# Gated cross-attention with experts on one core: mask and maximum in one VectorE instruction, exponentials from SBUF, scores in mid-round, eight P buffers

## What is computed

```python
q = (layernorm(x) @ Wq.T + bq)    # 32 x 16 heads x 128 x 8
k = (ctx @ Wk.T + bk)             # 32 x 16 heads x 120 x 8
v = (ctx @ Wv.T + bv)
scores = einsum('bhqd,bhkd->bhqk', q, k) / sqrt(8)
scores = where(mask == 0, -inf, scores)      # one 128 x 120 mask for all batches and heads
attn = softmax(scores, axis=-1)
x = x + tanh(g_xattn) * (einsum('bhqk,bhkd->bhqd', attn, v) @ Wo.T + bo)
x = x + tanh(g_ffn) * experts(layernorm(x))
```

## Time and profile before

| | |
|---|---|
| median of 3 runs | 454.4 us (454.36 to 455.76) |
| span of the profiled execution | 428.0 us |
| median less that span | 26.4 us |
| attention stage, first maxima to last routing step of round 31 | 17.92 to 257.63 us |
| one steady group of four rounds (first matmul of V to that of the next group) | 109.24 to 139.10 us |

### The profile page before, as it was taken

How to read it: one execution, slowest core, us unless ns; L and a number is a source line. 1 busy time by engine, 2 the same in 40 slices (tenths; PEclk the granted TensorE clock), 3 DMA queues, 4 the chain that set the end, 5 groups by cost and what they waited for, 6 DMA issues and landing times.

```text
span 428.0 us, 12221 instructions
## 1 busy us (share of the span) xinstructions
PE 385.6 (90%) x4245; PEld 311.8 (73%) x4245; DVE 293.0 (68%) x1075; ACT 267.9 (63%) x828; POOL 256.9 (60%) x280
## 2 busy tenths in 40 slices
PE   2989999999999999999999999898999999999500
PEld 1556776877687777768777768887999999999500
DVE  4787887888788898888898987735752333333177
ACT  2367877878788887878778683323444445544254
POOL 5354536547879699698794455444677777645500
PEclk9999999999999999999999999989999999999955
DMA  3999999952000000000000186556869888885198
GB/s 83 232 266 412 412 412 395 232 109 58 21 27 15 23 20 14 28 15 16 28 16 20 35 248 220 163 164 178 224 181 294 243 295 275 288 277 181 37 311 278
DMA packets 47194, 72.20 MB, mean 169 GB/s; under 512 B 7974, under 2 KB 31662, under 8 KB 47134
## 3 DMA queue, kind: packets, MB, share of 16 engines
q1 hardware_dynamic: 42813, 62.44, 47.5%
q0 software_dynamic: 4320, 8.99, 5.9%
HBM read 41.94 MB, written 34.20 MB: 178 GB/s over the span
## 4 chain that ended last, share of the span: by engine, by line
PE 77%; DVE 9%; ACT 6%; DMA 3%; issue 3%; SPq 1%; POOL 1%; POOLq 0%; DVEq 0%; ACTq 0%
PE S L790 14%; PE S L670 7%; PE T L772 7%; PE U L772 7%; PE S L681 7%; PE O L702 6%; PE T L689 5%; PE U L689 5%; PE O L710 5%; ACT P L862 5%; DMA yg<-res 2%; PE S L796 2%; PE E L662 2%; DVE nmax L1158 1%; PE E L651 1%
## 5 line engine op out<-in xcount | busy, mean ns | idle before, releaser
L862 ACT ACTIVATE P<-S,nmax 128x120 f32<-128x120 f32 x512 | 137.1, 411 | 41.8 <-DVE nmax L1158 41.8
L1016 POOL DMA_INDIRECT zs<-z,posu x64 | 64.6, 1010 | 58.2 <-PE O L710 24.4
L1158 DVE TENSOR_REDUCE nmax<-S 128x4 f32<-128x480 f32 x128 | 75.2, 650 | 19.8 <-PE S L681 15.2
L1027 POOL DMA_INDIRECT res<-yo,dpos x71 | 68.0, 958 | 32.5 <-DVE yo L1343 17.8
L790 PEld LDWEIGHTS S<-wbuf,H 128*128 128x128 f32 x568 | 74.3, 193 | 3.4 <-issue 0.2
L790 PE MATMUL S<-wbuf,H 128*128 128x128 f32 x568 | 75.3, 277 | 0.0
L670 PE MATMUL S<-mb_r,I_r 128*128 128x480 f32 x128 | 63.7, 499 | 3.7 <-ACT P L862 2.6
L906 ACT ACTIVATE H<-T,wbuf 128x256 f32<-128x256 f32 (+1 forms) x82 | 31.7, 445 | 41.0 <-PE T L772 41.0
L906 ACT ACTIVATE H<-U,wbuf 128x256 f32<-128x256 f32 (+1 forms) x78 | 30.5, 449 | 38.5 <-PE U L772 38.4
L977 POOL TENSOR_SCALAR z<-X,mv,rstd 128x128 f32<-128x128 f32 x56 | 44.1, 793 | 10.3 <-PE O L710 7.1
L989 POOL TENSOR_SCALAR Kb<-Kt,hm 128x480 f32<-128x480 f32 x28 | 41.4, 1487 | 13.0 <-PE O L745 6.3
(11 more groups left out here) (174 smaller groups left out, 628.9 us busy)
## 6 DMA issues: line engine op xcount, KB each, us to landing
wbuf<-wpk SPq DMA_DIRECT2D x40, 578.0 KB, 4.5
zs<-zero SPq DMA_DIRECT2D x1, 17952.0 KB, 61.6
yg<-res SPq DMA_DIRECT2D x16, 256.0 KB, 4.2
zin<-zs SPq DMA_DIRECT2D x31, 132.0 KB, 4.3
wpk<-in_w SPq DMA_DIRECT2D x1, 2048.0 KB, 57.9
wpk<-in_w SPq DMA_DIRECT2D x8, 256.0 KB, 8.2
out<-X SPq DMA_DIRECT2D x16, 128.0 KB, 3.5
ctx_sb<-in_ctx SPq DMA_DIRECT2D x1, 1440.0 KB, 16.5
```

Source lines behind the costliest of these rows:

```text
L862: ins = nc.scalar.activation(P[:, n % 4, j, :], a[:, j * LK:(j + 1) * LK], ACT.Exp, bias=nmax[:, n % 4, j:j + 1])
L1016: nc.gpsimd.indirect_dma_start(out=zs, out_offset=bass.IndirectOffsetOnAxis(ap=posu[:, F, k, i:i + 1], axis=0), in_=z2[:, F % 2, i, :], in ...
L1027: nc.gpsimd.indirect_dma_start(out=res, out_offset=bass.IndirectOffsetOnAxis(ap=dpos[:, n % NDP, h:h + 1], axis=0), in_=yo[:, n % NYO, h, ...
L1158: v.tensor_reduce(nmax[:, n % 4, :], Sb[n % NHG][:, 0:HG * LK].rearrange("p (j k) -> p j k", j=HG), AX_X, ALU.max, negate=True).then_inc(m ...
```

## The change

- The mask matmuls go, with the two casts that made their operands. The first scores matmul of a bank now starts it.
- In place of `row_max`, DVE has `masked(n)`: four instructions, each (S + mask bias) x -1 written into P, 120 columns, and the minimum of these written into `nmax`. It waits for the scores and for the transposes that read this buffer of P before.
- The exponentials read and write P in SBUF, exp(-P + nmax); P and `nmax` have eight buffers. `s_free` is replaced by `p_done` (exponentials done) for the transposes and by `max_done` for the banks.
- PE issues `scores(k + 1)` after the transposes of g = 1 in round k; the first entry of a round moves behind g = 2 and the second behind g = 3. On DVE `masked` of batch k+1 stands after `unload` and the two copies, a first entry behind it. On ACT the second entry is evicted in the next round after the first exponentials, the first entry between the two copies.
- `yg` is laid into P, and the counts of `prep_dve` fall by two.

The diff without lines that only rename a wait or change a count:

```diff
@@ -74,6 +74,7 @@
 NYG = 6
 NPT = 8
+NPB = 8
 ZROW = 8 * ZW
...
@@ -271,7 +272,6 @@
 
         I = sb("I", [128, 128])
-        I_r = sb("I_r", [128, 128], F32R)
         iota_sb = sb("iota_sb", [128, NE])
...
@@ -288,7 +288,6 @@
         hm = sb("hm", [128, HG])
         mbias = sb("mbias", [128, LK])
-        mb_r = sb("mb_r", [128, LK], F32R)
         mask_i = sb("mask_i", [128, LK], I32)
...
@@ -328,8 +327,8 @@
         Vm = sb("Vm", [LK, 2, GB * HG, NHG * (32 + DK)])
         oneV = sb("oneV", [LK, NHG, 32])
-        nmax = sb("nmax", [128, 4, HG])
-        P = sb("P", [128, 4, HG, LK])
+        nmax = sb("nmax", [128, NPB, HG])
+        P = sb("P", [128, NPB, HG, LK])
         PT = sb("PT", [LK, NPT, HG * LQ])
...
@@ -380,7 +379,7 @@
         own_i = sb("own_i", [128, NDP * TH], I32)
         own = sb("own", [128, NDP, TH])
-        yg = sb("yg", [128, NYG, UB, 2, D])
+        yg = P[:].rearrange("p n j k -> p (n j k)")[:, 0:NYG * UB * 2 * D].rearrange("p (n i k d) -> p n i k d", n=NYG, i=UB, k=2)
 
...
@@ -662,31 +661,24 @@
                 last.then_inc(e_ready, 1)
 
-            def add_mask(n):
-                if n < NHG:
-                    freed(pe, FIRST[n], 0)
-                else:
-                    pe.wait_ge(s_free, n - NHG + 1)
-                mm(Sb[n % NHG][:, 0:HG * LK].rearrange("p (j k) -> p j k", j=HG), I_r[:],
-                   mb_r[:].unsqueeze(1).broadcast_to((128, HG, LK)), start=True, stop=False)
-
             def scores(k):
                 G, i = divmod(k, GB)
                 if i == 0:
                     freed(pe, "Q", G)
                     pe.wait_ge(kb_done, G + 1)
                     pe.wait_ge(kb_first, 1)
+                wait(pe, max_done, NHG * k)
                 for g in range(NHG):
                     r = slice(32 * g, 32 * g + 32)
                     mm(Sb[g][:, 0:HG * LK].rearrange("p (j k) -> p j k", j=HG), Q[r, G % 2, i * LQ:(i + 1) * LQ],
-                       Kb[r, G % 2, :, i * LK:(i + 1) * LK], start=False, stop=True,
+                       Kb[r, G % 2, :, i * LK:(i + 1) * LK], start=True, stop=True,
                        tile_position=(32 * g, 0)).then_inc(s_ready, 1)
 
             def transposes(n):
-                pe.wait_ge(s_free, n + 1)
+                pe.wait_ge(p_done, n + 1)
                 copied(pe, prior_t(n))
                 for j in range(HG):
-                    last = nc.tensor.transpose(t_bank(n)[0:LK, j * LQ:(j + 1) * LQ], P[:, n % 4, j, :], I[:])
+                    last = nc.tensor.transpose(t_bank(n)[0:LK, j * LQ:(j + 1) * LQ], P[:, n % NPB, j, :], I[:])
                 last.then_inc(t_ready, 1)
...
@@ -809,25 +801,25 @@
                 old, new = 0 <= k - 1 < B, k + 1 < B
                 first, second = entries_of(k)
-                if first:
+                if first and k >= B:
                     entries[first[0]](first[1])
                 if old:
                     values(k - 1)
                     sums(k - 1)
                 for g in range(NHG):
                     pair(ks[2 * g:2 * g + 2])
-                    if new:
-                        add_mask(NHG * (k + 1) + g)
                     if k < B:
                         transposes(NHG * k + g)
-                    if g == 1 and second:
+                    if g == 1 and new:
+                        scores(k + 1)
+                    if g == 2 and first and k < B:
+                        entries[first[0]](first[1])
+                    if g == (3 if k < B else 1) and second:
                         entries[second[0]](second[1])
                 if k == 0:
-                    pe.wait_ge(prep_dve, 16)
+                    pe.wait_ge(prep_dve, 14)
                     pe.wait_ge(b2t_done, 1)
                     mm(Ob[:, 0:D], bvb[:], wo_sb[:], start=True, stop=True).then_inc(bvo_ready, 1)
-                if new:
-                    scores(k + 1)
                 if k == OPEN:
...
@@ -837,12 +829,8 @@
             k_entry(0)
             z_entry(0)
-            pe.wait_ge(prep_dve, 5)
-            add_mask(0)
-            add_mask(1)
+            pe.wait_ge(prep_dve, 1)
             q_entry(0)
-            add_mask(2)
-            add_mask(3)
             scores(0)
...
@@ -856,12 +844,10 @@
             def exps(n):
                 act.wait_ge(max_done, n + 1)
-                wait(act, t_ready, n - 3)
-                a = Sb[n % NHG]
                 for j in range(HG):
-                    ins = nc.scalar.activation(P[:, n % 4, j, :], a[:, j * LK:(j + 1) * LK], ACT.Exp,
-                                               bias=nmax[:, n % 4, j:j + 1])
-                ins.then_inc(s_free, 1)
+                    a = P[:, n % NPB, j, :]
+                    ins = nc.scalar.activation(a, a, ACT.Exp, bias=nmax[:, n % NPB, j:j + 1], scale=-1.0)
+                ins.then_inc(p_done, 1)
 
...
@@ -916,13 +902,18 @@
                 G, p = divmod(k, GB)
                 first, second = entries_of(k)
+                before = entries_of(k - 1)[1] if k else None
                 if k < B:
                     exps(NHG * k)
-                pair(ks[0:1])
+                if before and k <= B:
+                    evict(*before)
+                if first and k >= B:
+                    pair(ks[0:1])
+                    evict(*first)
+                else:
+                    pair(ks[0:1])
                 if k < B:
                     exps(NHG * k + 1)
-                if first:
-                    evict(*first)
                 if k == 0:
...
@@ -935,11 +926,13 @@
                 if k < B:
                     exps(NHG * k + 3)
-                if second:
+                if second and k >= B:
                     evict(*second)
                 pair(ks[4:5])
                 if k < B:
                     copy_pt(NHG * k + 2)
+                    if first:
+                        evict(*first)
                     copy_pt(NHG * k + 3)
...
@@ -1150,13 +1143,14 @@
                 ins.then_inc(step, 1)
 
-            def row_max(n):
+            def masked(n):
 
                 dve.wait_ge(s_ready, n + 1)
-                if n >= 4:
-                    dve.wait_ge(s_free, n - 3)
-                v.tensor_reduce(nmax[:, n % 4, :], Sb[n % NHG][:, 0:HG * LK].rearrange("p (j k) -> p j k", j=HG),
-                                AX_X, ALU.max, negate=True).then_inc(max_done, 1)
+                wait(dve, t_ready, n - NPB + 1)
+                for j in range(HG):
+                    ins = v.tensor_tensor_reduce(P[:, n % NPB, j, :], Sb[n % NHG][:, j * LK:(j + 1) * LK], mbias[:], -1.0, 3e38,
+                                                 ALU.add, ALU.min, nmax[:, n % NPB, j:j + 1])
+                ins.then_inc(max_done, 1)
 
...
@@ -1374,22 +1368,24 @@
                 G, p = divmod(k, GB)
                 first, second = entries_of(k)
+                if first and first[0] in taken and k >= B:
+                    taken[first[0]](first[1])
+                if 0 <= k - 1 < B:
+                    unload(k - 1)
                 if k < B:
-                    for g in range(NHG):
-                        row_max(NHG * k + g)
+                    copy_pt(NHG * k)
+                    copy_pt(NHG * k + 1)
                 if k == 0:
                     dve.wait_ge(in_const, N_CONST)
                     dve.wait_ge(tanh_done, 2)
                     made(v.tensor_scalar(wo_sb[:], wo_sb[:], tx[:, 0:1], None, ALU.mult), False)
                     made(v.tensor_scalar(bo_sb[:], bo_sb[:], tx[:, 0:1], None, ALU.mult), False)
                     made(v.tensor_scalar(bvb[:], one_f[:], bv_sb[:, 0:1], None, ALU.mult), False)
-                if first and first[0] in taken:
+                if k + 1 < B:
+                    for g in range(NHG):
+                        masked(NHG * (k + 1) + g)
+                if first and first[0] in taken and k < B:
                     taken[first[0]](first[1])
-                if 0 <= k - 1 < B:
-                    unload(k - 1)
-                if k < B:
-                    copy_pt(NHG * k)
-                    copy_pt(NHG * k + 1)
                 if k == 0:
...
@@ -1446,7 +1442,6 @@
             stats(stat1, mv1[:, 0], 0, ln1_step)
             dve.wait_ge(in_id, 16)
-            made(v.tensor_copy(I_r[:], I[:]), False)
             dve.wait_ge(in_first, N_FIRST)
...
@@ -1460,7 +1455,6 @@
             dve.wait_ge(in_mask, 16)
             made(v.tensor_scalar(mbias[:], mask_i[:], 0.0, MASKED, ALU.is_equal, ALU.mult))
-            made(v.tensor_copy(mb_r[:], mbias[:]), False)
             freed(dve, "K", 0)
...
@@ -1482,6 +1476,8 @@
             made(v.tensor_tensor(upto[:], it[:, 0:NE].unsqueeze(1).broadcast_to((128, NE, NE)),
                                  it[:, 0:NE].unsqueeze(2).broadcast_to((128, NE, NE)), ALU.is_le))
+            for g in range(NHG):
+                masked(g)
             dve.wait_ge(const_done, 3)
...
```

(8 more changed lines are left out.)

## The result

The changed kernel takes 463.1 us (median; 459.9 to 465.6) where the kernel before takes 454.4 (453.5 to 455.8) beside it: ratio 1.0171, 95% interval 1.0115 to 1.0226. Slower, as forecast, by 8.7 us instead of 30.

The account below looks back on a forecast made before the run. PE bounds the kernel before; VectorE was to bound the changed one. Its stage, 127.5 + 136.7 + 6.2 = 270.4 us, is 30.7 over 239.7, less 0.7 at the start: span 458.0 plus 26.4 outside gives 484; range 446 to 506.

Parts of the forecast that it names:

- Price of the new instruction: VectorE's masked instruction: pitch p from start to start, 0.202 us body plus 0.065 for the minimum, 0.267; 512 take 136.7 us.
- The other work of VectorE: Attention stage: VectorE's 202.7 us less 75.2 us of old reductions leaves 127.5 us.
- Idle that stays: VectorE in attention: of 37.0 us idle, 30.8 us of waits go and 6.2 us stay.
- rival 1: VectorE's new instruction: minimum comes for nothing, p at most 0.21; 451 us at 0.202; chance 0.27, with or without rival 2 (ScalarE bound).
- the wait is already met: PE's scores moved to mid-round: they wait for the last maximum, which VectorE made a round earlier, so no delay.
- Evictions that move cost nothing: Moved evictions on ScalarE: same instructions, covered by ScalarE's 1.5 us to spare a round.
- VectorE as last engine: Attention rounds: VectorE's sum sets the time, a steady round about 8.3 us, PE idle 2 us in it.
- PE's relief: Four mask matmuls leave PE: 1.15 us a round, so PE alone needs 6.31 instead of 7.46 us.
- ScalarE from SBUF: The 512 exponentials: pitch 0.29 us against 0.244 from PSUM, 6.76 us a round, costing nothing under VectorE's sum.
- rival 4: PE's clock drops from 2.4 to 1.2 GHz as PE idles; round nears 12.6 us, time 620; chance 0.03.
- Base: The 26.4 us between the profiled span of 428.0 and the median of 454.4 lie outside the span and stay.
- rival 5: Mid-round scores come late and VectorE waits 1 us a round: 32 us on top of rival 1; chance 0.03.

Follow-up runs that it names:

- e1: Changed kernel with POOL making a group's last two key blocks ahead of the expert rows; 455.38 us, 1.0040 to the kernel before.
- e4: Changed kernel with early key blocks and VectorE taking RANK after the first head group's four new instructions; 453.58 us, 0.9995 to the kernel before.
- e8: e7 with a round's two entries set apart, the first behind the scores and evicted ahead of ScalarE's copies; 447.70 us, 0.9879.
- e10: e8 with only head group 1 masked on PE; 445.13 us, 0.9834 to the kernel before.
- e9: e4 with a round's two entries set apart, no mask on PE; 450.03 us, 0.9949 to the kernel before.
- e7: e4 with head groups 0 and 1 given mask matmul, row_max and exponentials from PSUM again; 454.11 us, 1.0008 to the kernel before.
- e5: Kernel before with only row_max, masks and the exponentials' source exchanged, scores at the round's end, four P buffers; 471.62 us, 1.0416.
- after: The changed kernel as profiled, no further edit; median 463.1 us, ratio 1.0171 to the kernel before, profiled span 461.2 us.
- c0: The kernel before, unedited, run and profiled once more; 454.13 us, ratio 0.9992, span 451.4 us.
- e2: Changed kernel with VectorE's two copies of transposes ahead of unload; 465.91 us, 1.0234 to the kernel before.

## Why the prediction was right in sign and wrong in size

- **Price of the new instruction: wrong, and this is the step that failed.** The forecast added 0.065 us to the body because side operands and the pair MATCH, FIND showed an extra. p is 0.203. 512 x (0.267 - 0.203) = 33 us of VectorE work that never came: 28.57 us in a group instead of the 33 forecast. Those rows have one more input per partition, or hand a value to the instruction behind; the new one has one more output, which here is handed over beside the next body. They were the nearest rows, but of another kind. That the minimum is an instruction of its own did not make the price real, as the prediction had concluded. The bound from the body (0.202) was exact.
- **The other work of VectorE: right.** 127.5 + 103.4 = 230.9 by the steps, measured 230.25 to the last routing step.
- **Idle that stays: wrong, the other way.** The prediction let 6.2 us stay and called all new waits met; 19.0 us stayed. With p = 0.202 it gave a stage of 237.1 us and 451 as rival 1. The stage took 249.3; the 12 us more are these 12.8. The failed step is "the wait is already met": it looked at one semaphore of the moved scores, not at `kb_done`. "Evictions that move cost nothing" failed too: ScalarE had time, but the eviction stands between two users of one bank. e1 and e4 together price the two waits at 5.8 us of attention; e8 to e10 price the entries at 0.5 points without masks on PE (e4 to e9) and 1.3 with half of them there (e7 to e8), 2.7 and 7.0 us of attention in the traces.
- **VectorE as last engine: wrong as put.** In the steady groups its price alone made it so: it stood 2.5 of 31.1 us, and e7 took 13 us of work from it for no gain in time. In the first group it was right (busy 33.93 of 34.94), and that cost 3.7 us. Both signs of failure that the prediction named came: p is under 0.21, and VectorE's idle is 0.6 us a round.
- **PE's relief: too high.** The chain share gave 1.15 us a round for the masks, PE 6.31. PE is busy 27.38 / 4 = 6.85. Its busy time fell by 2.48 us in a steady group, 0.16 us a mask matmul instead of 0.29 (0.19 over the stage to the last sums). Here the share of the chain overstated what goes with a line. This decided nothing in the changed kernel.
- **ScalarE from SBUF: right** (0.286 against 0.29), and right that it hides in the new order. e5 shows the cost without that cover.
- **The clock (rival 4): right in kind, but seldom.** It did not become the rule. In attention it fell in after for some 3 us behind the stop of 2.55 us; in e1 it fell for 7 us more behind stops of 1.47 and 0.33. The prediction's reason, that pieces well under 1 us are harmless, does not hold always: in c0 the clock fell behind stops of 0.77 and 0.40 us (last section). And it differs between executions of one kernel.
- **Base: wrong.** Only 2.0 of the 26.4 us lay outside the span of c0, which is 23.4 us longer, 3.1 of them in attention. It did little harm to the forecast of the time, since both kernels have them.
- **Range:** 446 to 506 held the time. It lay in the gap that I gave a chance of 8 in 100, between rival 1 and the forecast: rival 1's price together with new waits, a combination that had no case of its own (rival 5 put them at 32 us). That the range held is luck in part: one error of 33 us too much and one of 13 too little.

What stays open: how much of the first group's 3.7 us an edit could win back; why the clock falls behind a stop in one execution and not behind the same stop in another; and why "another core or an unknown queue" holds the experts' stage for some 20 us in some places and not in others. No run changed that stage.

## What to carry to other kernels

When work is moved forward in a queue, list every semaphore in front of it and look up in the trace when each was met in the old place; the least margin (here that of the key blocks of another engine) sets the price, and it need not belong to the semaphore that the change touches. Two users of one buffer set back to back put the engine that empties it on the chain of waits, as ScalarE in e7, though it has time to spare. Give two nearly full engines a divisible task in the proportion that evens them out, and look at the groups in which one of them has other work besides: masks of two head groups in four on PE 0.988, of one 0.983, of none 0.995 (with 3 us of it from one stop and the clock behind it). The kernel before (all four on PE, 1.000) has another order and is no point of this series.

## What the runs showed of the hardware

- A custom VectorE instruction of 128x120 with one operand in PSUM and an accumulated minimum repeats every 0.203 us. The accumulator read (0.08 us) is a record of its own and costs no time between two such bodies.
- 128x120 exponentials in place in SBUF repeat every 0.286 us on ScalarE, from PSUM every 0.244. The Trainium skill ("Perfetto Trace Analysis", section "Optimizing Scalar/DVE Operations") has about 93 ns of overhead in SBUF and 51 in PSUM for ScalarE: the difference of 42 ns is the measured one. Its 125 ns for VectorE on PSUM would, as an estimate from that page, make the new instruction 0.25 us; the 0.203 measured decides.
- TensorE's clock stands at either of its two levels, and a stop does not settle which. Behind stops of 2.55 us (after) and 3.50 us (e2) it fell to 1.2 GHz, behind 2.06 us (e9) for 7 us, behind 1.47 and 0.33 us (e1, from about 260.5 us) and behind 0.77 and 0.40 us (c0, 260.00 to 263.58 us, mean 0.55). Behind 1.56 us (after, 134.65) and behind the same 1.47 and 0.33 us in after it did not fall.

```profile
260.18 1.94 PE L702 MATMUL O<-PT,Vm 120*32 120x128 f32 x32 [0.40 <-issue]
```

These 32 matmuls in c0 take 1.94 us; at 2.4 GHz they take 1.08.
